# Attention with a maximum: one row reduction over two PSUM banks, and exponentials of 512 columns

## What is computed

```python
def _L3_xattn_ref(query, context, mask, ...):
    q, k, v = ...                      # 16 heads of depth 8
    scores = jnp.einsum('bhid,bhjd->bhij', q, k) * scale
    scores = jnp.where(mask[:, None, None, :], -jnp.inf, scores)
    attn = jax.nn.softmax(scores, axis=-1)
    out = jnp.einsum('bhij,bhjd->bhid', attn, v)
    ...
```

## Time and profile before

| | us |
|---|---|
| median of 3 runs | 8553.93 (8548.58 to 8557.4) |
| profiled execution, its own time | 8551.03 |
| its span | 8549.2 |
| VectorE busy in the span | 6960.8 (81%) |
| TensorE busy | 5875.3 (69%) |
| ScalarE busy | 4913.9 (57%) |
| the three calls of `attend_with_max`, first row fill to last copy of the sums | 221 to 1384, 1616 to 2779, 7183 to 8346 |

### The profile page before, as it was taken

The page is one execution under the profiler, slowest core; times in us unless marked ns, Lnnn a source line. Parts: engine busy times, 40 slices in busy tenths (PEclk is TensorE's granted clock), DMA queues, the critical chain, the costliest instruction groups (busy, mean ns, idle before and its releaser), DMA issues. The chain is left out here.

```text
span 8549.2 us, 101651 instructions
## 1 busy us (share of the span) xinstructions
PE 5875.3 (69%) x35301; PEld 1769.4 (21%) x35301; DVE 6960.8 (81%) x14058; ACT 4913.9 (57%) x5921; POOL 669.4 (8%) x345
## 2 busy tenths in 40 slices
PE   5588887478888444533554777767788774788887
PEld 1011112111111111100110111144444441111113
DVE  5899991599995699999997999966766675999953
ACT  3177775057778344433444999944444550577782
POOL 1000000000000000000000000043433440000000
PEclk8599998689999555555556999978888885899998
DMA  7100001300000100000002000000000002000001
GB/s 217 28 2 16 16 1 36 77 3 15 16 2 1 24 8 8 8 8 8 8 4 47 16 16 3 1 28 13 13 9 13 11 4 55 3 15 16 2 1 45
DMA packets 111753, 174.94 MB, mean 20 GB/s; under 512 B 14665, under 2 KB 94357, under 8 KB 106254
## 3 DMA queue, kind: packets, MB, share of 16 engines
q1 hardware_dynamic: 111278, 168.91, 7.8%
HBM read 125.66 MB, written 43.21 MB: 20 GB/s over the span
## 5 line engine op out<-in xcount | busy, mean ns | idle before, releaser
L1008 DVE TENSOR_REDUCE a_partial<-a_row 128x1 f32<-128x494 f32 x4992 | 3021.5, 664 | 215.1 <-PE a_row L888 146.2
L974 ACT ACTIVATE a_prob<-a_score 128x1024 f32<-128x1024 f32 x2448 | 2360.5, 1021 | 606.5 <-PE a_score L901 606.2
L888 PE MATMUL a_row<-a_kg,a_qn 54*128 54x494 bf16 x4992 | 1027.8, 409 | 762.7 <-DVE a_partial L1008 660.9
L516 ACT COPY m_rows<-m_score 128x1536 f32<-128x1536 f32 (+1 forms) x640 | 760.9, 1250 | 919.3 <-PE m_score L495 804.1
L913 PE MATMUL a_acc<-a_prob,a_v_all 128*9 128x512 f32 x9792 | 1282.5, 596 | 1.7 <-ACT a_prob L974 1.4
L573 DVE MAX8 m_cand<-m_rows 128x8 f32<-128x192 f32 x4352 | 1220.7, 343 | 13.6 <-ACT m_rows L516 13.2
L495 PE MATMUL m_score<-m_kb,m_qb 54*128 54x512 bf16 (+1 forms) x1664 | 765.9, 608 | 309.4 <-ACT m_rows L516 243.8
L782 DVE SCALAR_TENSOR_TENSOR a_prob<-a_score,a_prob 128x1024 f32<-128x1024 f32 x816 | 924.6, 1211 | 50.3 <-ACT a_prob L758 50.3
L758 ACT ACTIVATE a_prob<-a_score,a_lower 128x1024 f32<-128x1024 f32 x816 | 865.4, 1110 | 72.9 <-PE a_score L701 21.2
L901 PE MATMUL a_score<-a_qb,a_kg 54*128 54x512 bf16 x4896 | 761.1, 379 | 34.7 <-ACT a_prob L974 20.8
L888 PEld LDWEIGHTS a_row<-a_kg,a_qn 54*128 54x128 bf16 x4992 | 241.9, 94 | 2357.4 <-DVE a_partial L1008 2232.4
(11 more groups left out here) (305 smaller groups left out, 5859.1 us busy)
## 6 DMA issues: line engine op xcount, KB each, us to landing
a_kg<-kst SPq DMA_DIRECT2D x64, 306.0 KB
kst<-kv_parts SPq DMA_DIRECT2D x48, 384.0 KB, 3.9
a_v_all<-vst SPq DMA_DIRECT2D x4, 3672.0 KB, 40.7
vst<-kv_va SPq DMA_DIRECT2D x48, 288.0 KB, 4.1
a_kg<-kst SPq DMA_DIRECT2D x64, 204.0 KB
e_cb<-comb SPq DMA_DIRECT2D x25, 512.0 KB
a_kg<-kst SPq DMA_DIRECT2D x64, 102.0 KB
qst<-q_parts SPq DMA_DIRECT2D x24, 256.0 KB, 3.2
```

What stands on the lines that cost most here:

```text
L516: act.copy(rows[i][:, c * CH:c * CH + n], score[(i * NCH + c) % 2][:, 0:n]).then_inc(copied, 1)
L888: pe.matmul(row[(use + half) % 3][:, 0:CW], qn[u % 2][rows, pair, i * P:(i + 1) * P], kg[u // NQC % 2][rows, pair, c * CW:(c + 1) * CW], s ...
L974: act.activation(prob[tile % PROBS][:, pair, :, :], score[use % 2][:, :, :], ACT.Exp).then_inc(slot_out, 1)
L1008: dve.tensor_reduce(partial[:, u % 2, 2 * item + half, c:c + 1], row[use % 3][:, 0:CW], AX, ALU.max).then_inc(reduced, 1)
```

## The change

All of it is in `attend_with_max`. The banks are divided anew: `row` becomes two tiles of two banks (it was three of one), `score` three tiles of one bank (it was two of two).

- A row pair fills the two banks of one `row` tile, counts as one filling (one increment of `filled`), and VectorE reduces both banks under one instruction, 2 x 494 columns into two maxima. That makes 832 reductions a call where there were 1664. A pair may be filled when the reduction two before it has ended.
- A score pair takes two of the three single banks, each matmul with its own increment of `scored`, and ScalarE takes four exponentials of 512 columns a tile instead of two of 1024. The cast of the turned queries is likewise two of 512. A score pair may be made when the exponential of the last slot but one has ended.
- The order on TensorE is another: the second score pair of the present tile, then `turn` and `heads`, `sums` of the tile before, the first score pair of the next tile, and then all row pairs of the tile.

```diff
-        score = [m.ps(f"score{i}", [P, 2, QC]) for i in range(2)]
+        score = [m.ps(f"score{i}", [P, QC]) for i in range(3)]
-        row = [m.ps(f"row{i}", [P, QC]) for i in range(3)]
+        row = [m.ps(f"row{i}", [P, 2, QC]) for i in range(2)]
...
         def bank_use(pair_fill, tile):
-            return pair_fill + heads_before(tile)
+            return pair_fill // 2 + heads_before(tile)
...
                     for half in range(2):
-                        pe.matmul(row[(use + half) % 3][:, 0:CW], qn[u % 2][rows, pair, i * P:(i + 1) * P],
-                                  kg[u // NQC % 2][rows, pair, c * CW:(c + 1) * CW], start=True,
-                                  stop=True).then_inc(filled, 1)
+                        last = pe.matmul(row[use % 2][:, half, 0:CW], qn[u % 2][rows, pair, i * P:(i + 1) * P],
+                                         kg[u // NQC % 2][rows, pair, c * CW:(c + 1) * CW], start=True, stop=True)
+                    last.then_inc(filled, 1)
...
             def scores(tile, pair):
-                use = slot_use(tile, pair)
+                use = slot_use(tile, 2 * pair)
                 if use >= 2:
                     pe.wait_ge(slot_out, use - 1)
                 for half in range(2):
-                    last = pe.matmul(score[use % 2][:, half, :], kg[u // NQC % 2][rows, pair, k * P:(k + 1) * P],
-                                     qb[u % 2][rows, pair, :], start=True, stop=True)
-                last.then_inc(scored, 1)
+                    pe.matmul(score[(use + half) % 3][:, :], kg[u // NQC % 2][rows, pair, k * P:(k + 1) * P],
+                              qb[u % 2][rows, pair, :], start=True, stop=True).then_inc(scored, 1)
...
             for tile in range(UNITS * KT):
+                scores(tile, 1)
                 if k == TURN_AT and u + 1 < UNITS:
                     turn(u + 1)
                 if k == HEADS_AT and u:
                     heads(u - 1)
-                pairs = row_pairs(tile)
-                row_fills(tile, pairs[:1])
                 if tile:
                     sums(tile - 1)
-                row_fills(tile, pairs[1:])
                 if tile + 1 < UNITS * KT:
-                    for pair in range(2):
-                        scores(tile + 1, pair)
+                    scores(tile + 1, 0)
+                row_fills(tile, row_pairs(tile))
...
-                for pair in range(2):
-                    use = slot_use(tile, pair)
+                for j in range(G):
+                    use = slot_use(tile, j)
                     act.wait_ge(scored, use + 1)
                     if tile >= PROBS:
                         act.wait_ge(summed, tile - PROBS + 1)
-                    act.activation(prob[tile % PROBS][:, pair, :, :], score[use % 2][:, :, :], ACT.Exp).then_inc(slot_out, 1)
+                    act.activation(prob[tile % PROBS][:, j // 2, j % 2, :], score[use % 3][:, :],
+                                   ACT.Exp).then_inc(slot_out, 1)
...
-                    for half in range(2):
-                        dve.tensor_reduce(partial[:, u % 2, 2 * item + half, c:c + 1], row[use % 3][:, 0:CW], AX,
-                                          ALU.max).then_inc(reduced, 1)
+                    dve.tensor_reduce(partial[:, u % 2, 2 * item:2 * item + 2, c], row[use % 2][:, :, 0:CW], AX,
+                                      ALU.max).then_inc(reduced, 1)
```

More of the change, by code:

```diff
@@ L834, in bank_use, with slot_use @@
         def bank_use(pair_fill, tile):
-            return pair_fill + heads_before(tile)
-        def slot_use(tile, pair):
+            return pair_fill // 2 + heads_before(tile)
+        def slot_use(tile, j):
             u, k = tile // KT, tile % KT
-            return 2 * tile + pair + 1 + u + (1 if k > TURN_AT and u + 1 < UNITS else 0)
+            return G * tile + j + 2 * (1 + u + (1 if k > TURN_AT and u + 1 < UNITS else 0))
         def turn_use(u):
-            return 0 if u == 0 else slot_use((u - 1) * KT + TURN_AT, 1) + 1
+            return 0 if u == 0 else slot_use((u - 1) * KT + TURN_AT, G - 1) + 1
         @block.sync
@@ L924, in turn @@
                 for pair in range(2):
-                    pe.matmul(score[use % 2][:, pair, :], identb[:, :], qn[u % 2][:, pair, :], start=True, stop=False)
+                    slot = score[(use + pair) % 3]
+                    pe.matmul(slot[:, :], identb[:, :], qn[u % 2][:, pair, :], start=True, stop=False)
                     for i in range(QT):
-                        last = pe.matmul(score[use % 2][:, pair, i * P:(i + 1) * P],
+                        last = pe.matmul(slot[:, i * P:(i + 1) * P],
                                          place[:, pair * QT + i, :, :].rearrange("p s r -> p (s r)"), identb[:, :],
                                          start=False, stop=(i == QT - 1))
-                last.then_inc(scored, 1)
+                    last.then_inc(scored, 1)
             def heads(u):
@@ L936, in heads @@
                 pe.wait_ge(ob_ready, u + 1)
-                pe.wait_ge(reduced, use - 2)
+                pe.wait_ge(reduced, use - 1)
                 for i in range(QT):
-                    last = pe.transpose(row[use % 3][:, i * P:(i + 1) * P], ob[:, i * P:(i + 1) * P], ident[:, :])
+                    last = pe.transpose(row[use % 2][:, 0, i * P:(i + 1) * P], ob[:, i * P:(i + 1) * P], ident[:, :])
                 last.then_inc(filled, 1)
@@ L945, in _ @@
             turn(0)
-            for pair in range(2):
-                scores(0, pair)
+            scores(0, 0)
             for tile in range(UNITS * KT):
                 u, k = tile // KT, tile % KT
+                scores(tile, 1)
                 if k == TURN_AT and u + 1 < UNITS:
@@ L973, in exponentials @@
                         act.wait_ge(summed, tile - PROBS + 1)
-                    act.activation(prob[tile % PROBS][:, pair, :, :], score[use % 2][:, :, :], ACT.Exp).then_inc(slot_out, 1)
+                    act.activation(prob[tile % PROBS][:, j // 2, j % 2, :], score[use % 3][:, :],
+                                   ACT.Exp).then_inc(slot_out, 1)
             def keep_queries(u):
                 use = turn_use(u)
-                act.wait_ge(scored, use + 1)
                 if u >= 2:
                     act.wait_ge(summed, (u - 1) * KT)
-                act.copy(qb[u % 2][:, :, :], score[use % 2][:, :, :]).then_inc(slot_out, 1)
+                for pair in range(2):
+                    act.wait_ge(scored, use + pair + 1)
+                    act.copy(qb[u % 2][:, pair, :], score[(use + pair) % 3][:, :]).then_inc(slot_out, 1)
             def keep_sums(u):
@@ L1050, in _ @@
                 search(tile)
-            heads(UNITS - 1, UNITS * FILLS + UNITS - 1)
+            heads(UNITS - 1, UNITS * FILLS // 2 + UNITS - 1)
 def project(nc, att, wo, bo, gate, xs, ident, tag):
```

23 lines of the change are left out of this document (11 added, 12 removed).

## The result

The changed kernel takes 8495.67 us (median of 4 runs, 8493.82 to 8498.0) against 8552.7 us before (4 runs, 8548.58 to 8557.4): a ratio of 0.9933, 95% interval 0.9916 to 0.9951. That is 57 us less. The profiled execution took 8498.0 us, its span is 8496.2.

The account below looks back on a forecast made before the run. The prediction took a loop through one reduction and the sums, 2.44 us a tile, to bound the search. Prologue -30, search -22, tail +29 make -23 us a call, -69 for three: 8554 - 69 = 8485 us, range 8430 to 8530.

Parts of the forecast that it names:

- The two durations: In the changed kernel, a reduction of 988 columns takes about 1.18 us and an exponential of 512 takes 595 ns.
- The loop: Search and tail: exponential, second score pair, sums, next first score pair and back to exponential set 2.37 us a tile.
- Prologue: Start of a call: fills pass under reductions, a pair takes 1.10 us instead of 1.36; 114 pairs, -30 us a call.
- Tail: End of a call, without search: 2.37 us a tile instead of 1.86; 56 tiles, +29 us a call.
- Search: Full-search phase: a unit takes 126.9 us instead of 130.05; 352 tiles are 6.9 units, -22 us a call.
- the clock stays: TensorE's granted clock stays at 1.00, as in layer 2's attention with the same sums, scores and waits between them.
- The idle of 0.86 us: Kernel before, ahead of the second row pair: taken as a sign that TensorE is held back in its order of work.
- the third rival: The reduction saves nothing: two hold VectorE up to 2.66 us a tile; mostly 8530 to 8570, far end 8870; chance 0.07.
- VectorE's pace: Rival: VectorE's own work sets the full search's pace at 2.20 us a tile; near 8300 us; chance 0.08.
- Dearer exponentials: Rival: exponentials cost more inside the loop, 687 ns making it 2.46 us a tile; 8540 to 8600 us; chance 0.13.

Follow-up runs that it names:

- three other kernels: Kernel before with only the new TensorE order, 9040.4 us; changed kernel with the old order, 8883.3 us; changed kernel with zero-tensor bias on every exponential, 8641.9 us.
- the kernel with two reductions: Changed kernel with each row pair reduced by two instructions of 494 columns instead of one over both banks: 8533.8 us, ratio to before 0.9974.
- the longer exponential: Changed kernel with a tensor of zeros as bias of every exponential, each 0.090 us longer: 8641.9 us in the profiled execution, without an interval.
- The kernel with wide tiles in the last unit: Changed kernel with last-unit score pairs in the two row tiles, exponentials of 1024 and the old order there: 8425.6 us, ratio 0.9849.
- The kernel with the order alone: Kernel before with only the changed order of TensorE, banks and instructions as before: 9040.4 us, ratio 1.0573.

## Why the prediction was right

Forecast 8485, measured 8496; direction and mechanism as forecast, the size within 11 us.

- *The two durations.* 1.18 us for the reduction was 1182 ns, 595 ns for the exponential was 594. The row at 1024 columns, also in PSUM and also in several runs, priced the first; the difference of two other rows, taken off the exponential of 1024, priced the second. The formula of the Trainium skill ("ScalarE: Activation LUTs", section "What ACT_TABLE_LOAD costs"), 613 ns, was 19 ns too much for a read from PSUM.
- *The loop.* 2.37 forecast, 2.37 and 2.38 measured in search and tail. The same working gave 2.87, 2.79 and 2.46 for three other kernels, and each was met to 0.01. This, and the unmoved tile with VectorE's work 0.13 longer, show the loop rather than argue it.
- *Prologue*: -30 forecast, -30.6 measured. Only 7.3 of them are the merged instruction's (135.6 us with two reductions); the other 23.3 come with the tiles of two banks, which let a fill pass under a reduction. *Tail*: +29 for 56 tiles forecast, +27.8 for 55 measured. Here the new loop gives back nearly all that the prologue gains.
- *Search*: -22 forecast, -14.4 measured; this is the term that was mis-sized. A unit of 126.9 us was forecast; an undisturbed one takes 127.3 (the placing and the turn together 2.9 over an ordinary tile against 2.75 forecast, the two places with a third row pair 1.0 and 1.2 against 1.0 each), and one before takes 130.0. It gains 2.7 instead of 3.15, which makes 3 of the 7.6 us a call that are missing; 4 more are the clock's. And "the clock stays" was wrong at the turns: 9 of 18 tiles were 1.0 to 1.6 us longer, 11.4 us in all. The reason given, that layer 2's attention holds 2.4 GHz with similar waits, was about ordinary tiles, and for them and the tail it held (granted clock 1.00). It said nothing of the special tiles.
- *The size.* By the phases the three terms missed by +23, -2 and -4 us over three calls, 17 together: -52 where -69 was forecast. The medians differ by 57 and the profiled executions by 53, so that the miss of 11 owes some 5 us to the spread of the executions. That is luck, though small.
- *Two slips in the working.* The idle of 0.86 us ahead of the second row pair was read as a wait of TensorE; it is that of the weight loads while TensorE works on the sums, and it stands in the same place in the changed kernel (802.96). And the third rival took durations for distances: two instructions a pair hold VectorE 2.33 us a tile, not 2.66, as the kernel with two reductions shows, so its far end of 8870 was priced too high: that kernel took 8534.
- *The rivals.* VectorE's pace was refuted by the two reductions and the longer exponential. Dearer exponentials: 594 ns. A reduction that saves nothing: 1182 ns. That larger operations help where an engine is saturated (the Trainium skill, "Perfetto Trace Analysis", section "Optimizing Scalar/DVE Operations") holds here for the prologue, where VectorE is busy without a gap and the merged instruction saves 7.3 us a call; in the search VectorE was 97% busy and was still not what closed the tile.

## What to carry to other kernels

An engine that is busy 97% of the time need not set the pace: add up the loops of waits (end of A, start of B, and round to A again) and see whether one of them is the period; if it is, price the change as the loop that it leaves behind. Price it for each phase, since a ring of buffers that suits the phase with two kinds of work can cost in the phase with one, where buffers of the other kind lie idle and can be lent. Where TensorE waits in a special tile, look at the granted clock there: two waits that were harmless apart cost a stretch at half clock in half of the places where they met.

## What the runs showed of the hardware

- The granted clock of TensorE fell to 1.2 GHz for a few microseconds in the middle of a phase at 2.4 GHz, at 9 of 18 like places of the changed kernel. The kernel with wide tiles in the last unit is the same up to there and has 9 too, but not all at the same turns; the one with two reductions has 12. At the fall shown above, it had been busy 0.67 and then 1.23 of 2 us. At the turn of the unit before it (594 to 598 us), where the clock stays at 1.00, it is busy 1.17 and 0.73; at the turn of the kernel before, 0.75 and 1.35, and the clock stays at 1.00 at all 18:

```profile
594.00:596.00 2.00, 1.17 (x12) 0.12 (x4) 1.83 (x7) 1.79 (x4) 0.00 (x0) 1.00 0.00 0
596.00:598.00 2.00, 0.73 (x5) 0.24 (x6) 2.00 (x3) 0.95 (x3) 0.00 (x0) 1.00 0.00 0
...
628.00:630.00 2.00, 0.75 (x7) 0.22 (x10) 1.93 (x6) 1.48 (x2) 0.00 (x0) 1.00 0.02 4
630.00:632.00 2.00, 1.35 (x14) 0.21 (x6) 1.97 (x4) 0.82 (x1) 0.00 (x0) 1.00 0.00 0
```

The first two lines are of the changed kernel, the last two of the kernel before. The kernel with the order alone fell after 1.19 and 1.27 of 2 us. What decides where the clock falls stays open.
- One VectorE instruction reads across two PSUM banks: 988 columns in 1182 ns, against 2 x 664 ns for two of 494, and 1.09 us from start to start against 2 x 0.58.
- ScalarE reads 512 columns from PSUM every 0.50 us back to back and 1024 every 0.93.
